# A four-layer network on one core: the wait of 52 slot writes, and the place of 14 small VectorE operations

## The chip, the cores and the metric

The kernel runs on one core of a Trainium2 chip. The metric is the device time of one execution in microseconds (us). TensorE (PE) multiplies matrices, VectorE (DVE), ScalarE (ACT) and GpSimd (POOL) do the elementwise work, and transfers are issued from SyncE (SP), ScalarE and GpSimd. Indirect transfers, whose target rows are taken from a table, are issued from GpSimd.

## The reference

There are 2048 tokens (4 sequences of 512) of width 512, and four blocks in a row, each added to its input: a selective scan over a context, a mixture of 32 experts with 4 per token, cross attention, and a second mixture of 32 experts with 8 per token. The change lies in the second mixture. Cut to what matters, it is:

```
x = layernorm(x)
scores = sigmoid(x @ router_w)                       # 2048 x 32
masked = the scores + bias of the 4 best of 8 groups of experts
top_k_index = top_k(masked, 8)
tkw = scores[top_k_index]; tkw = 2.5 * tkw / sum(tkw)
xs = repeat(x, 8)[argsort(experts)]                  # 16384 rows, expert by expert
down = (silu(xs @ w_gate) * (xs @ w_up)) @ w_down    # each row with its expert's weights
routed = sum over a token's 8 rows of down * tkw
shared = silu(x @ sw_gate) * (x @ sw_up) @ sw_down
out = residual + routed + shared
```

## The kernel before

The second mixture has two stages, one after the other with a barrier between: `route_stage` (with L = 1) and `expert_stage1`.

The routing stage computes the router's scores, picks the experts, and gives each of the 16384 pairs of token and expert a slot in a buffer in HBM, `xs1`. The slots of an expert are consecutive and padded to halves of 64 rows; two halves make a tile of 128 rows, and there are 144 tiles. `tcum` is the running count of halves up to each expert. TensorE meanwhile computes the shared expert: for each of four batches `b` of 512 tokens four chunks (`chunk(b, f)`, a gate and an up product), whose results VectorE multiplies (`product(b, f)`, line 1004), and then `down(b)` (line 1265), which needs all four products of its batch and whose four results VectorE adds to the residual (`add_shared(b)`, line 1066). VectorE does these between the steps of its own chain: the choice of experts, the slots of the first 512 tokens (`first_slots`), the table of experts per tile (`te`, `tei`), and the slots of the other three batches (`slots_of(b)`). Each engine executes its instructions in the order in which they are written.

The rows are written to their slots by 128 indirect transfers from GpSimd, each of 128 rows of 529 float32 (271 KB): 16 tiles of tokens times the 8 experts of a token. `SLOT_ORDER` puts the first batch of tokens first (32 writes), and then, for all other tokens, the 8 ranks one after another, starting with the lowest expert number, 12 writes a rank. The first 76 writes (`EARLY`) are issued in the routing stage, the last 52 at the start of the expert stage (line 1904). Write `n` raises the counter of lane `n % 4`. Before it issues write `n`, GpSimd waits until write `n - reach` has landed; `reach` is 2 in the routing stage and 3 in the expert stage.

The expert stage works through the 144 tiles. ScalarE issues the loads of rows, four tiles (a group) at a time, into two buffers; VectorE turns them (line 2058); TensorE multiplies with the gate and up weights (`up`, line 2141), turns the hidden rows (line 2150) and multiplies with the down weights (`down`, line 2163); ScalarE scales the result into one of 16 output tiles `e_yo` (line 1965); GpSimd adds its two halves to the output in HBM by two indirect transfers (line 1911). GpSimd does this only after all 128 slot writes have landed:

```
for n in range(EARLY, len(SLOT_ORDER)):
    write_slots(pool, D, route, n, 3)
for lane in range(LANES1):
    pool.wait_ge(written[lane], 16 * NT * K1 // LANES1)
```

Tile `t` takes the place of tile `t - 16`. VectorE (`addressed`, line 2087) therefore waits on the counter `added`, which GpSimd raises when it comes to the add of the tile two further on and finds the older adds landed. The adds of the first three tiles wait for one another; later ones wait only where halves of two experts meet.

The rows of the first six groups may not be loaded before enough slot writes have landed. How many is enough depends on how many experts lie in the group's rows: VectorE counts them from `tcum` into the table `rows_held` (14 operations on a single partition, lines 1190 to 1197), and ScalarE reads the table before each of these loads (`rows_written`). For the routing of these inputs the six groups need 56, 68, 80, 92, 104 and 116 writes.

SyncE loads the weights of the experts, one expert ahead of a ring of four, when the expert whose place they take is done.

Of the kernel before, what the change touches and what calls it, by code (L numbers as in the profile page):

```python
# [17 lines left out]
ALU = mybir.AluOpType  # L18
# [683 lines left out]
    step(dve.tensor_tensor(gt, gt, eq, ALU.add))  # L702


def write_slots(pool, D, route, n, reach):

    t, k = SLOT_ORDER[n]
    written = route["written"]
    if n >= reach:
        pool.wait_ge(written[(n - reach) % LANES1], 16 * ((n - reach) // LANES1 + 1))  # L710
    pool.indirect_dma_start(D["xs1"][:, :], bass.IndirectOffsetOnAxis(route["scat"][:, t, k:k + 1], 0),  # L711
                            route["xn"][:, t, 0:H + 2 * K1 + 1], None, bounds_check=NSLOT1 - 1, oob_is_err=False)\
        .then_inc(written[n % LANES1], 16)


def route_stage(nc, c, I, D, x, L, route, ahead=None, out=None):
# [10 lines left out]
    with ExitStack() as ctx:  # L727
# [79 lines left out]
        with nc.Block() as block:  # L807
# [65 lines left out]
            def _(pool):  # L873
# [14 lines left out]
                if L == 0:  # L888
                    for t in range(NT):
                        pool.wait_ge(sem["idx"], 1 + t // TB + 1)  # L890
                        for k in range(K):
                            n = t * K + k
                            if n >= 2:
                                pool.wait_ge(written[(n - 2) % LANES], 16 * ((n - 2) // LANES + 1))
                            pool.indirect_dma_start(slots[:, :], bass.IndirectOffsetOnAxis(scat[:, t, k:k + 1], 0),
                                                    xn[:, t, 0:XU], None, bounds_check=nslot - 1, oob_is_err=False)\
                                .then_inc(written[n % LANES], 16)
                    for lane in range(LANES):
                        pool.wait_ge(written[lane], 16 * NT * K // LANES)
                else:  # L900
                    for n in range(EARLY):
                        if n < TB * K and n % K == 0:
                            pool.wait_ge(sem["idx0"], 1 + n // K + 1)
                        if n == TB * K:
                            pool.wait_ge(sem["idx"], 1 + B - 1)
                        write_slots(pool, D, route, n, 2)

            @block.scalar
            def _(act):
# [49 lines left out]
            def _(dve):  # L959
# [188 lines left out]
                if L == 1:  # L1148
# [6 lines left out]
                    step(dve.tensor_scalar(route["ends"][0:1, 1:], ti[0:1, :], 1, None, ALU.arith_shift_right), wait=False)  # L1155
                    step(dve.tensor_scalar(te[:, :], te[:, :], float(E - 1), None, ALU.min))
                    dve.tensor_copy(tei[:, :], te[:, :]).then_inc(sem["eid"], 1)
                if L == 0:
                    slots_of(0, base1, lambda: product(0, FIRST + 2))
                    dve.wait_ge(sem["gate"], 1 + 1)  # L1160
# [18 lines left out]
                else:  # L1179
# [7 lines left out]
                    product(1, 3)  # L1187
                    slots_of(3, base1)
                    add_shared(1)
                    for g in range(GROUPS_HELD):  # L1190
                        step(dve.tensor_scalar(past[0:1, :], tcum[0:1, :], float(2 * RING1 * (g + 1) - 1), None, ALU.is_le))
                        step(dve.tensor_reduce(tf[0:1, g:g + 1], past[0:1, :], AX_X, ALU.add))
                    held = tf[0:1, 0:GROUPS_HELD]
                    per_rank = 16 * TB * (B - 1) // LANES1
                    step(dve.tensor_scalar(held, held, float(K1 - 1), None, ALU.min))
                    step(dve.tensor_scalar(route["rows_held"][:, :], held, float(per_rank), float(16 * TB * K1 // LANES1 + per_rank),
                                           ALU.mult, ALU.add), wait=False)
                    for b in range(2, B):
                        for f in range(FC):
                            product(b, f)  # L1200
# [606 lines left out]
def expert_stage1(nc, c, I, D, x, route, W, out):  # L1807
# [3 lines left out]
    with ExitStack() as ctx:  # L1811
# [59 lines left out]
        with nc.Block() as block:  # L1871
# [26 lines left out]
            def _(pool):  # L1898
# [2 lines left out]
                pool.iota(after_i[:, :], [[32, NTILE1 // 2], [32, 2], [0, 2]], base=-32, channel_multiplier=0).then_inc(sem["iota"], 1)  # L1901
                pool.iota(within_i[:, :], [[32, NTILE1 // 2], [0, 2]], base=0, channel_multiplier=0).then_inc(sem["iota"], 1)
                for n in range(EARLY, len(SLOT_ORDER)):
                    write_slots(pool, D, route, n, 3)
                for lane in range(LANES1):
                    pool.wait_ge(written[lane], 16 * NT * K1 // LANES1)
                pool.wait_ge(stored, 16 * (B + 2))
# [1361 lines left out]
```

## Time and profile before

| | us |
|---|---|
| three runs | 2952.52, 2956.33, 2965.47 |
| median | 2956.33 |
| the profiled execution | 2952.52 |
| its span | 2950.8 |

| engine | busy, us | share of the span |
|---|---|---|
| TensorE | 2628.0 | 89% |
| VectorE | 1542.0 | 52% |
| GpSimd | 1295.0 | 44% |
| ScalarE | 1032.9 | 35% |

The span is the time from the first to the last instruction in one profiled execution. The second mixture's routing stage begins near 1881 us, its expert stage near 2093 us. Of an issued transfer, an engine's row shows the issuing alone; how long it takes to land is seen only from who waits for it. "issue" as a releaser is time in which the engine waited for nothing that the profile shows.

### The profile page before, as it was taken

Reading aid. Unit: us, or ns where it says so; the run is one execution under the profiler, and the core shown is the slowest. Engines: PE = TensorE matmul, PEld = TensorE weight load, DVE = VectorE, ACT = ScalarE, POOL = GpSimd, SP = SyncE. Lnnn points to the kernel's source line nnn. Section 1 sums busy time; section 2 is a strip of 40 time slices with the busy share of each in tenths; the row PEclk is TensorE's granted clock in tenths of the full one; section 3 lists DMA queues with packets and bytes.
Section 4 is the critical chain, followed back from the end, with each engine's and each line's share of the span. In section 5 each row is a group of like instructions: output and inputs, shape, how many; then the busy total and the mean of one; then the engine's idle time right before and its main releaser. Section 6 shows DMA issues by size and latency. Waiting matters only on the chain. (4 is left out here: it accounts for less than half of the span.)

```text
span 2950.8 us, 40989 instructions
## 1 busy us (share of the span) xinstructions
PE 2628.0 (89%) x11315; PEld 1086.3 (37%) x11318; DVE 1542.0 (52%) x2668; ACT 1032.9 (35%) x1305; POOL 1295.0 (44%) x933
## 2 busy tenths in 40 slices
PE   5889876699999987768999999899798999999997
PEld 2333432244444433323343333334233333333332
DVE  7999999741100033126566665451344555555553
ACT  4647464120000001013443433200244555555553
POOL 2767656312400022114664643135445556545556
PEclk8999999999999999889999999899899999999999
DMA  3333222301210269975047300144786877787865
GB/s 127 116 98 109 83 62 74 130 36 37 88 33 14 73 218 343 340 205 141 1 121 200 96 1 1 51 175 169 214 233 131 166 157 128 160 199 162 171 115 79
DMA packets 361927, 373.15 MB, mean 126 GB/s; under 512 B 85810, under 2 KB 268403, under 8 KB 361778
## 3 DMA queue, kind: packets, MB, share of 16 engines
q1 hardware_dynamic: 202210, 239.03, 25.8%
q0 software_dynamic: 45520, 93.26, 14.9%
q10 hardware_dynamic: 114048, 39.16, 6.7%
q8 instruction: 58, 0.95, 0.1%
q14 instruction: 91, 0.75, 0.1%
HBM read 231.96 MB, written 152.14 MB: 130 GB/s over the span
## 5 line engine op out<-in xcount | busy, mean ns | idle before, releaser
L1911 POOL DMA_INDIRECT out_x<-e_yo,e_dest x288 | 418.9, 1455 | 327.7 <-DMA out_x<-e_yo,e_dest 249.7
L2141 PE MATMUL e_psg<-e_wgu,e_xsT 128*64 x1152 | 522.3, 596 | 17.0 <-DVE e_xsT L2058 17.0
L2141 PE MATMUL e_psg<-e_cgu,e_xsT 128*64 128x512 f32 x1152 | 522.3, 596 | 0.0
L295 POOL TENSOR_TENSOR hc<-hs,bcst 128x1024 f32<-128x1024 f32 x128 | 300.8, 2351 | 179.0 <-DVE ps_b L515 171.5
L640 PE MATMUL ps_y<-hc,ident 128*128 128x512 f32 x512 | 241.1, 609 | 88.1 <-POOL hc L295 87.8
L1984 ACT ACTIVATE e_cgu<-e_wgu 128x2048 f32 x144 | 275.2, 1912 | 66.2 <-issue 63.1
L521 DVE TENSOR_TENSOR_SCAN hs<-dA,ps_b 128x1024 f32<-128x1024 f32 x128 | 292.6, 2286 | 8.1 <-ACT dA L425 3.9
L2163 PE MATMUL e_pso<-e_wd,e_hT 128*64 x576 | 272.2, 595 | 14.8 <-DVE e_hT L2063 13.1
L2163 PE MATMUL e_pso<-e_cd,e_hT 128*64 128x512 f32 x576 | 272.2, 595 | 0.0
L2141 PEld LDWEIGHTS e_psg<-e_wgu,e_xsT 128*64 128x64 f32 x1152 | 154.7, 138 | 268.2 <-issue 268.1
L937 ACT ACTIVATE r_sg<-r_ps_g 128x512 f32<-128x512 f32 x60 | 35.8, 597 | 525.2 <-PE r_ps_g L1246 512.6
L1265 PE MATMUL r_ps_t<-r_wd,r_h 128*128 128x512 f32 x480 | 210.9, 600 | 9.4 <-DVE r_h L1004 5.1
L1004 DVE TENSOR_TENSOR r_h<-r_ps_u,r_sg 128x512 f32<-128x512 f32 x60 | 41.4, 691 | 316.7 <-PE r_ps_u L1246 299.6
L711 POOL DMA_INDIRECT slots_in<-r_xn,scat x128 | 126.9, 992 | 173.1 <-DMA slots_in<-r_xn,scat 101.2
L425 ACT ACTIVATE dA<-dt,a_neg 128x511 f32<-128x511 f32 x256 | 165.2, 713 | 102.9 <-DVE hs L521 97.8
L2751 DVE TENSOR_REDUCE a_nm<-a_ps 128x2 f32<-128x992 f32 x128 | 146.1, 1185 | 88.3 <-PE a_ps L2995 87.9
L2513 ACT ACTIVATE a_pt<-a_ps 128x1024 f32<-128x1024 f32 (+1 forms) x128 | 126.2, 1022 | 181.3 <-PE a_ps L3012 120.5
L2068 DVE TENSOR_TENSOR e_h<-e_psg,e_sg 128x256 f32<-128x256 f32 x144 | 61.1, 424 | 244.0 <-ACT e_sg L1958 212.8
L640 PEld LDWEIGHTS ps_y<-hc,ident 128*128 128x128 f32 x512 | 92.8, 191 | 231.1 <-POOL hc L295 137.4
L1965 ACT ACTIVATE e_yo<-e_pso,e_wrow 128x512 f32<-128x512 f32 x144 | 99.0, 688 | 223.9 <-PE e_pso L2163 176.0
L2058 DVE STREAM_TRANSPOSE e_xsT<-e_xs 128x512 f32<-128x512 f32 x144 | 173.0, 1201 | 5.8 <-DMA e_xs<-slots_in 5.8
L2076 DVE COPY e_cd<-e_wd 128x1024 f32 x144 | 102.0, 708 | 133.7 <-PE e_pso L2163 107.7
(430 smaller groups left out, 4207.0 us busy)
## 6 DMA issues: line engine op xcount, KB each, us to landing
slots_in<-zeros SPq DMA_DIRECT2D x144, 256.0 KB, 2.3
e_xs<-slots_in ACTq DMA_DIRECT2D x144, 256.0 KB
bcst<-bc_rows SPq DMA_DIRECT2D x128, 256.0 KB, 4.2
e_wgu<-in_wg SPq DMA_DIRECT2D x32, 512.0 KB
e_wgu<-in_wu SPq DMA_DIRECT2D x32, 512.0 KB
e_wd<-in_wd SPq DMA_DIRECT2D x32, 512.0 KB
e_w<-in_wg SPq DMA_DIRECT2D x11, 1408.0 KB
e_w<-in_wu SPq DMA_DIRECT2D x11, 1408.0 KB
```

The lines of the kernel that those rows point to most:

```text
L295: pool.tensor_tensor(hc[:, it % 2, half(h), :], hs[:, it % 2, half(h), :], bc(bcst[:, q, 1, :], 1, HB), ALU.mult).then_inc(sem["hc"], 1)
L425: i = act.activation(dA[:, it % 2, t, 1:], dt[:, b % 2, t, 1:], ACT.Exp, scale=a_neg[:, n, t:t + 1])
L521: dve.tensor_tensor_scan(hs[:, it % 2, half(h), :].rearrange(flat), dA[:, it % 2, half(h), :].rearrange(flat), ps_b[:, :, :].rearrange(fla ...
L640: i = pe.matmul(ps_y[:, t, :], c["ident"][:, :], hc[:, it % 2, t, :], start=False, stop=False, skip_group_check=True)
L711: pool.indirect_dma_start(D["xs1"][:, :], bass.IndirectOffsetOnAxis(route["scat"][:, t, k:k + 1], 0), route["xn"][:, t, 0:H + 2 * K1 + 1], ...
L1265: i = pe.matmul(ps_t[:, j % 2, :], h[:, f, j * P:(j + 1) * P], wd[:, f, :], start=f == 0, stop=f == FC - 1)
L1911: pool.indirect_dma_start(out[:, :], bass.IndirectOffsetOnAxis(dest[:, q, s:s + 1], 0), yo[half(s), q, :], None, bounds_check=T + 2 * P - ...
L1984: act.activation(cgu[:, q % 2, :, :], wgu[:, bass.ds(e % RING, 1), :, :].rearrange("p o k n -> p (o k) n"), ACT.Copy).then_inc(sem["cgu"], 1)
L2058: dve.transpose(xsT[:, q % 2, :, :].rearrange("p k (s j) -> p k s j", j=DQ), xs[:, q // RING % 2, part, :].rearrange("p s (i k) -> p k s i ...
L2141: j = pe.matmul(ps_g[half(s), q % 2, :], xsT[:, q % 2, k, half(s)], w, start=k == 0, stop=k == KH - 1, tile_position=(0, s * HALF), skip_g ...
L2163: j = pe.matmul(ps_o[half(s), q % 2, :], hT[:, q % 2, a, half(s)], w, start=a == 0, stop=a == NW - 1, tile_position=(0, s * HALF), skip_gr ...
L2751: dve.tensor_reduce(nm[:, i % 8, 2 * z:2 * z + 2], ps[:, at:at + 2, 0:S2], AX_X, ALU.max, negate=True)\
```

## The change

Two things are edited. `write_slots` loses its parameter `reach`: all 128 writes now wait for the second write before. And the 14 operations that fill `rows_held` are written directly behind the one that hands over the table `tei`, in place of behind `add_shared(1)`.

```
-def write_slots(pool, D, route, n, reach):
+def write_slots(pool, D, route, n):
...
-    if n >= reach:
-        pool.wait_ge(written[(n - reach) % LANES1], 16 * ((n - reach) // LANES1 + 1))
+    if n >= 2:
+        pool.wait_ge(written[(n - 2) % LANES1], 16 * ((n - 2) // LANES1 + 1))
...
-                        write_slots(pool, D, route, n, 2)
+                        write_slots(pool, D, route, n)
...
                     dve.tensor_copy(tei[:, :], te[:, :]).then_inc(sem["eid"], 1)
+                    for g in range(GROUPS_HELD):
+                        step(dve.tensor_scalar(past[0:1, :], tcum[0:1, :], float(2 * RING1 * (g + 1) - 1), None, ALU.is_le))
...
                 if L == 0:
...
                     add_shared(1)
-                    for g in range(GROUPS_HELD):
-                        step(dve.tensor_scalar(past[0:1, :], tcum[0:1, :], float(2 * RING1 * (g + 1) - 1), None, ALU.is_le))
...
                     for b in range(2, B):
...
-                    write_slots(pool, D, route, n, 3)
+                    write_slots(pool, D, route, n)
```

On GpSimd, at the start of the expert stage, before the change (`e_sloti` to `e_withini` are number tables; the counters of the four lanes stand under the names `m_win`, `m_weights`, `m_xin` and `m_ctxin`, in the order of lanes 0 to 3):

```order
L1901 IOTA e_afteri 1x288
L1902 IOTA e_withini 1x144
L711 DMA slots_in<-r_xn,scat 18432x544 [waits m_weights]
L711 DMA slots_in<-r_xn,scat 18432x544 [waits m_xin]
L711 DMA slots_in<-r_xn,scat 18432x544 [waits m_ctxin]
L711 DMA slots_in<-r_xn,scat 18432x544 [waits m_win]
```

On GpSimd, at the same place, in the changed kernel:

```order
L1901 IOTA e_afteri 1x288
L1902 IOTA e_withini 1x144
L711 DMA slots_in<-r_xn,scat 18432x544 [waits m_xin]
L711 DMA slots_in<-r_xn,scat 18432x544 [waits m_ctxin]
L711 DMA slots_in<-r_xn,scat 18432x544 [waits m_win]
L711 DMA slots_in<-r_xn,scat 18432x544 [waits m_weights]
```

The writes are the same and stand in the same order; each, from number 76 on (lane 0), waits for the lane two behind its own in place of three.

On VectorE, in the routing stage behind the table `tei`, before the change (`r_te` and `r_tei` are that table, `r_h` the products of the shared expert, `r_seg`, `r_k` and `r_hit` the slots of batch 1):

```order
L1156 TENSOR_SCALAR r_te<-r_te 128x3
L1157 CAST r_tei<-r_te 128x3
L1004 TENSOR_TENSOR r_h<-r_ps_u,r_sg 128x512 x2
L1011 TENSOR_TENSOR r_seg<-r_pos,r_base 128x128
L1018 COPY r_seg<-r_sc 128x128
```

On VectorE, at the same place, in the changed kernel (the last of the six pairs of lines 1159 and 1160, and what follows):

```order
L1159 TENSOR_SCALAR r_past<-r_tcum 1x32
L1160 TENSOR_REDUCE r_tf<-r_past 1x1
L1163 TENSOR_SCALAR r_tf<-r_tf 1x6
L1164 TENSOR_SCALAR rows_held<-r_tf 1x6
L1004 TENSOR_TENSOR r_h<-r_ps_u,r_sg 128x512 x2
L1011 TENSOR_TENSOR r_seg<-r_pos,r_base 128x128
L1018 COPY r_seg<-r_sc 128x128
```

The two products of batch 0, `product(0, 2)` and `product(0, 3)`, now stand behind 14 more operations.

## Rows read from the trace of the kernel before

**Rows 1.** The page's chain that ended last, by line, shares of the span.
```profile
PE e_psg L2141 12%; PE e_pso L2163 6%; DMA out_x<-e_yo,e_dest 2%; PE e_psh L2150 1%; POOL out_x L1911 0%; POOLq L1939 0%; POOLq L1937 0%; POOLq L1928 0%; POOLq L80 0%; POOLq L1911 0%; DVE e_xsT L2058 0%; DMA slots_in<-r_xn,scat 0%; ACT e_yo L1965 0%; POOLq L79 0%; DVEq L2072 0%
```

**Rows 2.** Stretches: us, busy us by engine, granted PE clock, DMA share, GB/s.
```profile
core 0: us, PE busy (x) PEld busy (x) DVE busy (x) ACT busy (x) POOL busy (x), PEclk, DMA share, GB/s
2214.00:2226.00 12.00, 0.42 (x4) 0.30 (x4) 2.83 (x8) 0.38 (x1) 3.90 (x3) 0.67 0.31 36
2300.00:2900.00 600.00, 600.00 (x3442) 231.24 (x3440) 321.23 (x862) 320.36 (x323) 331.17 (x228) 1.00 0.77 155
```

**Rows 3.** VectorE in order of time: start us, us, what, [idle before <-releaser].
```profile
2222.03 0.23 DVE L2087 SCALAR_TENSOR_TENSOR e_mine<-e_rec,e_slot 128x8 f32<-128x8 f32 x1 [12.65 <-POOLq L1932]
```

**Rows 4.** TensorE in order of time, at the same place.
```profile
2225.66 1.11 PE L2163 MATMUL e_pso<-e_wd,e_hT 128*64 x1 [11.58 <-DVE e_hT L2063]
```

**Rows 5.** The chain of waits, 2190 to 2225 us: start us, us, what.
```profile
2196.76 6.38 issue
...
2217.94 3.74 DMA out_x<-e_yo,e_dest
```

**Rows 6.** GpSimd in order of time: slot writes of the expert stage.
```profile
2095.22 1.01 POOL L711 DMA_INDIRECT slots_in<-r_xn,scat  x1 [0.18 <-issue]
...
2102.62 0.98 POOL L711 DMA_INDIRECT slots_in<-r_xn,scat  x1 [3.81 <-DMA slots_in<-r_xn,scat]
...
2172.13 0.98 POOL L711 DMA_INDIRECT slots_in<-r_xn,scat  x1 [0.30 <-issue]
2173.42 0.98 POOL L711 DMA_INDIRECT slots_in<-r_xn,scat  x1 [0.30 <-issue]
...
2195.78 0.98 POOL L711 DMA_INDIRECT slots_in<-r_xn,scat  x1 [0.31 <-issue]
```

**Rows 7.** GpSimd in order of time: slot writes of the routing stage.
```profile
1947.36 0.98 POOL L711 DMA_INDIRECT slots_in<-r_xn,scat  x1 [3.54 <-DMA slots_in<-r_xn,scat]
1952.09 0.98 POOL L711 DMA_INDIRECT slots_in<-r_xn,scat  x1 [3.75 <-DMA slots_in<-r_xn,scat]
1954.31 0.98 POOL L711 DMA_INDIRECT slots_in<-r_xn,scat  x1 [1.24 <-issue]
...
2003.01 0.98 POOL L711 DMA_INDIRECT slots_in<-r_xn,scat  x1 [2.56 <-DMA slots_in<-r_xn,scat]
...
2082.00 0.98 POOL L711 DMA_INDIRECT slots_in<-r_xn,scat  x1 [0.76 <-DMA slots_in<-r_xn,scat]
2083.82 0.98 POOL L711 DMA_INDIRECT slots_in<-r_xn,scat  x1 [0.84 <-DMA slots_in<-r_xn,scat]
```

**Rows 8.** Stretches with slot writes, columns as in rows 2.
```profile
1942.00:1968.00 26.00, 25.21 (x52) 11.07 (x53) 10.60 (x30) 0.60 (x1) 7.98 (x9) 0.88 0.88 306
2073.00:2084.00 11.00, 11.00 (x27) 4.93 (x26) 2.07 (x3) 0.00 (x0) 6.07 (x7) 1.00 0.38 145
2095.00:2120.00 25.00, 15.51 (x72) 5.47 (x74) 9.92 (x24) 8.99 (x7) 10.08 (x11) 0.72 1.01 258
```

**Rows 9.** VectorE in order of time, in the routing stage.
```profile
1941.40 1.29 DVE L1004 TENSOR_TENSOR r_h<-r_ps_u,r_sg 128x512 f32<-128x512 f32 x2
...
1993.79 0.20 DVE L1038 COPY r_xn<-r_k 128x32 f32<-128x32 f32 x1
...
2002.56 0.16 DVE L1191 TENSOR_SCALAR r_past<-r_tcum 1x32 f32<-1x32 f32 x1
...
2005.30 0.16 DVE L1196 TENSOR_SCALAR rows_held<-r_tf 1x6 int32<-1x6 f32 x1
2008.87 0.69 DVE L1004 TENSOR_TENSOR r_h<-r_ps_u,r_sg 128x512 f32<-128x512 f32 x1 [3.41 <-PE r_ps_u L1246]
```

**Rows 10.** TensorE in order of time, `down(0)` and `down(1)`.
```profile
1942.79 16.80 PE L1265 MATMUL r_ps_t<-r_wd,r_h 128*128 128x512 f32 x32 [3.37 <-issue]
...
1987.91 14.00 PE L1265 MATMUL r_ps_t<-r_wd,r_h 128*128 128x512 f32 x32 [0.85 <-DVE r_h L1004]
```

**Rows 11.** GpSimd's first operation in the expert stage.
```profile
2092.83 0.24 POOL L1899 IOTA e_sloti<- 128x144 int32 x1 [8.03 <-POOLq L112]
```

**Rows 12.** ScalarE's queue: the loads of rows that it issues in tile 10.
```profile
2172.50 0.99 ACTq L1970 DMA_DIRECT2D e_xs<-slots_in  x2
```

More of the change, by code:

```diff
@@ L1157, in _ @@
                     dve.tensor_copy(tei[:, :], te[:, :]).then_inc(sem["eid"], 1)
+                    for g in range(GROUPS_HELD):
+                        step(dve.tensor_scalar(past[0:1, :], tcum[0:1, :], float(2 * RING1 * (g + 1) - 1), None, ALU.is_le))
+                        step(dve.tensor_reduce(tf[0:1, g:g + 1], past[0:1, :], AX_X, ALU.add))
+                    held = tf[0:1, 0:GROUPS_HELD]
+                    per_rank = 16 * TB * (B - 1) // LANES1
+                    step(dve.tensor_scalar(held, held, float(K1 - 1), None, ALU.min))
+                    step(dve.tensor_scalar(route["rows_held"][:, :], held, float(per_rank), float(16 * TB * K1 // LANES1 + per_rank),
+                                           ALU.mult, ALU.add), wait=False)
                 if L == 0:
@@ L1189, in _ @@
                     add_shared(1)
-                    for g in range(GROUPS_HELD):
-                        step(dve.tensor_scalar(past[0:1, :], tcum[0:1, :], float(2 * RING1 * (g + 1) - 1), None, ALU.is_le))
[L1192 to L1197, printed above, removed]
                     for b in range(2, B):
```

## The prediction

> **What bounds the kernel now.** I read four views in this order: the chain of waits, the stretches of the last stage, the order of time around its one long stall, and the order of time of the slot writes that stand behind that stall.
>
> The chain that ended last runs through TensorE in the routed experts of layer 1 [rows 1]. From 2300 to 2900 us TensorE is busy all of the time, 600.00 of 600.00 us, at a granted clock of 1.00 [rows 2]; a tile has 32 of its instructions, so the 3442 are 107.6 tiles of 5.58 us. Nothing there can be gained or lost except at the end. So what happens ahead of 2300 us is passed on to the end one for one, if it delays TensorE. In the stretch from 2214 to 2226 TensorE works 0.42 of 12 us [rows 2]. VectorE is idle for 12.65 us before `e_mine` of tile 16, released by GpSimd's line 1932 [rows 3], and TensorE's next `e_pso` then starts after 11.58 us idle, released by VectorE's `e_hT` [rows 4]. Line 1932 is the count `added`: tile 16 takes the place of tile 0 in the ring of 16 output tiles and needs tile 0's two adds, and GpSimd raises the count only when it comes to tile 2. GpSimd comes to its first add so late because it must first issue all 128 slot writes and see them land. The chain says so: 6.38 us from the last write to GpSimd's next step, then adds, one after another, the fourth at 2217.94 [rows 5]. Thus the end of the slot writes is on the path, with no slack: whatever is added to it, up to tens of us, TensorE waits for at tile 16, and whatever is taken away comes back only up to the 11.58 us stall.
>
> **Edit 1, the wait of the last 52 slot writes on the second write before, in place of the third.** The 52 writes of the last stage start at 2095.22 and the last at 2195.78: 51 steps in 100.56 us, 1.97 us each [rows 6]. Undisturbed, a step lasts 1.29 us there (2172.13 to 2173.42), the price of issuing alone, so three writes in flight cover the whole way to landing. Of the 51 steps 27 are of this kind (under 1.36 us); the other 24 wait for a landing, and all steps together lie 34.8 us above 51 x 1.29. The first 76 writes, in the routing stage, already wait for the second before: there the undisturbed step is 1.78 to 1.82 us, as from 2082.00 to 2083.82 [rows 7]. Two such steps, 3.56 us, are the time from a write's start to the start of the write that waits for it. So the floor of the new order is 51 x 1.78 = 90.8 us.
>
> On that floor come the disturbances. They are latencies, seen under loads of rows and weights: DMA share 1.01 at 2095 to 2120 us, against 0.38 at the clean writes [rows 8]. With three in flight 2095.22 to 2102.62 took 7.40 us from a write to the one that waits for it [rows 6]. With two in flight and a DMA share of 0.88 [rows 8], two steps are nearly as long: from 1947.36 over 1952.09 to 1954.31 they make 6.95 us [rows 7]. The latency in traffic thus hardly shrinks with one write less in flight, and two in flight share it by 2 and not by 3. I replayed the 52 starts: where a write's step was over 1.36 us, the latency of the third before it is the difference of their starts; elsewhere it is 3.56 us, or less where the next starts force it. Under a wait on the second before, latencies kept whole make 136.8 us (+36.2); the part over 3.56 us scaled by 0.8, 127.1 us (+26.5); by two thirds, 120.7 us (+20.2); by a half, 112.9 us (+12.3); no excess at all, 90.3 us (-10). Adding only the part of each old step that is over 1.78 us to the floor gives 115 us (+14.5). The latest consistent latencies everywhere give 153 us (+52.5). The value that I take is 122 us, +21.5: latencies in traffic almost whole, less what the last ten or so writes gain, which now start when TensorE has stopped and its rows and weights are no longer loaded.
>
> From the Trainium skill, DMA: Bandwidth & Descriptors, section "Queues, rings and completion order": a DMA engine serves its queue rows in turn, a packet at a time. By that rule the latency of a write in traffic is made by the other queues and stays when fewer writes are in flight, and the sum would take the +36.2 us of the replay; the 6.95 us with two in flight [rows 7] agrees.
>
> Behind the last write, the 6.38 us to GpSimd's next step [rows 5] were in full traffic. A clean landing is 3.56 us from the start of the write, 2.58 us from the end of its 0.98 us of issuing, so up to 3.8 us come back; I take -2. The four adds behind stand as they are: 4.5 us apart, waiting for each other's landing, not for traffic. TensorE's stall grows from 11.6 to over 30 us. The clock after such a stall is read from rows: after 11.58 us idle the first product pairs go at half clock, mean granted 0.67 over 2214 to 2226 [rows 2], and after the pause ahead of this stage TensorE also starts at half clock. I take +1 for a longer slow start, bounds 0 and +2.6.
>
> Other waiters of the same counts: ScalarE asks for a part of the writes before it loads rows of groups 2 to 5 (80, 92, 104 and 116 writes for these inputs' routing), in tiles 2, 6, 10 and 14. Tile 10's loads are issued at 2172.50 [rows 12], tile 14's four tiles of 5.6 us later or more. In my replay the 104th write starts near 2167 us and the 116th near 2196 us, each a little before it is asked for; a wait of some us there would stop TensorE only in time that it otherwise spends waiting at tile 16. I count nothing; with latencies kept whole it would be up to 10 us, still hidden.
>
> **Edit 2, 14 small VectorE operations moved forward.** They count the experts of each group of rows. Before, they run from 2002.56 to 2005.46, 2.90 us, and VectorE then is idle 3.41 us until TensorE has a product: there they cost nothing, so taking them away gives nothing [rows 9]. Now they stand ahead of `product(0, 2)`, which starts at 1941.40 straight behind the operation before it [rows 9]. VectorE is late there: TensorE's `down(0)` starts at 1942.79 after 3.37 us idle [rows 10], because it needs the products of all four chunks. So 2.90 us go fully onto TensorE, whose work from there to the end of the stage has only gaps under 1 us. The end of the stage shifts with it: GpSimd's own writes of the first part are issued by 2084.80 [rows 7], yet its part of the last stage begins at 2092.83, after 8.03 us idle [rows 11]; GpSimd doesn't hold the change of stage, and starts 2.9 us later. The first expert weights are issued behind the id table, which isn't moved. Write 33, which waits for `slots_of(3)`, starts at 2003.01 [rows 7]; its table is done at 1993.99 [rows 9] and would be at 1996.9: 6 us of cover. TensorE's `down(0)` took 16.80 us at half clock for a part against 14.00 us for the next one [rows 10]; a longer gap may move that by 2 us either way, taken as 0. Edit 2: +2.9, bounds 0.9 and 4.9.
>
> **Sum.** +21.5 - 2 + 1 + 2.9 = +23.4 us. The profiled execution took 2952.52 us (span 2950.8), so 2976; the median of the three runs shown is 3.8 us above that one, and half of this makes the predicted 2978. A measurement of this kernel tells about 0.5%, 14.8 us, from no change.
>
> **The rivals.**
>
> *The writes were held by their own number.* If the latency in traffic is the queueing of a write behind its own two predecessors, one fewer in flight shortens it in proportion. The place is the stretch of 52 writes; the price is the floor, 90.3 us, 10 us less than now, and with edit 2 and the slow start the end comes at 2952.5 - 10 + 3.9 = 2946. It decides when the excess of latency falls below about a quarter of what it was, where the replay crosses 100.6 us. At the mean pace of the first 76 writes, 2.02 us a step, it would be 103 us and 2959. For it: a DMA share of 1.01 says throughput and not latency. Against it: 6.95 us with two in flight.
>
> *Latencies kept whole.* 136.8 us, perhaps 153: +36 to +52, with edit 2 and the clock 2992 to 3008. For it: the pairs in traffic of the first block. Against it: the last writes now run in quiet time.
>
> *A write lands in less than two issues.* Then the second before has landed whenever the next can be issued, edit 1 costs nothing, and only edit 2 is left: 2952.5 + 2.9 = 2955. Against it: the clean steps of 1.78 us in place of 1.29 [rows 6, 7], seen at a DMA share of 0.38. The Trainium skill, DMA: Bandwidth & Descriptors, section "Anatomy of one DMA", fits a GpSimd DMA as 2.0 us plus its bytes by 436 GB/s; for 271 KB an estimate of 2.6 us, which is this rival. The trace disagrees, with 3.56 us.
>
> *The path isn't as read.* If tile 16 is held by something other than the end of the writes, both edits hide: no change, 2953 to 2958. The chain of waits speaks against it.
>
> **Chances.** Forecast, +15 to +31 us (2967 to 2984): 0.57. Latencies whole or more: 0.21. Own number, at the floor or the first block's pace: 0.15. Landing in two issues: 0.02. Path misread: 0.05. The forecast's own low edge is just at the 0.5% bound, and some of its weight (0.04) falls inside. So slower 0.76, the same 0.22, faster 0.02. The range that leaves out about a tenth on each side is 2957 to 3002.
>
> **What the changed profile would show.** The 14 operations in one row near 1941 us and `down(0)` near 1945.7; GpSimd's last stage starting near 2095.7; undisturbed steps of 1.78 us between the 52 writes and a last start near 2220, not 2196; TensorE idle over 30 us in tile 16, and from there the same 5.58 us a tile to the end. A last write before 2200 would show the own-number rival; a stall at tile 16 as short as before, with late writes, would show that the path was misread; `down(0)` unmoved would refute edit 2's price.

## The result, and the profile after

| | before | after |
|---|---|---|
| median, us | 2957.26 (2952.52 to 2965.47) | 2981.47 (2976.76 to 2982.8) |
| the profiled execution, us | 2952.52 | 2986.22 |
| its span, us | 2950.8 | 2984.5 |

The change makes the kernel slower: ratio 1.0083, 95% interval 1.0067 to 1.0099, or 20 to 29 us. Forecast were 2978 us, 2957 to 3002, and 0.76 for slower. The profiled execution after is not one of the four behind the median. It is one of fifteen executions of the changed kernel on record, 2976.76 to 2988.6 us with a median of 2982.8, and lies 4.8 us above the median in the table.

GpSimd's slot writes of the expert stage after the change, in order of time (start us, us, what, [idle before <-releaser]), answer to [rows 5, 6, 11]:

```profile
2099.12 0.24 POOL L1899 IOTA e_sloti<- 128x144 int32 x1 [8.03 <-POOLq L112]
...
2101.50 1.01 POOL L711 DMA_INDIRECT slots_in<-r_xn,scat  x1 [0.18 <-issue]
2102.82 0.98 POOL L711 DMA_INDIRECT slots_in<-r_xn,scat  x1 [0.30 <-issue]
2109.15 0.98 POOL L711 DMA_INDIRECT slots_in<-r_xn,scat  x1 [5.35 <-DMA slots_in<-r_xn,scat]
...
2233.17 0.98 POOL L711 DMA_INDIRECT slots_in<-r_xn,scat  x1 [1.60 <-DMA slots_in<-r_xn,scat]
2234.79 0.98 POOL L711 DMA_INDIRECT slots_in<-r_xn,scat  x1 [0.64 <-issue]
2238.58 1.50 POOL L1911 DMA_INDIRECT out_x<-e_yo,e_dest  x1 [2.81 <-issue]
```

The 52 writes start from 2101.50 to 2234.79, 133.3 us in place of 100.6. The third write of the row starts 7.65 us after the first, on which it waits. With three in flight the fourth started 7.40 us after the first [rows 6]: the latency is the same, and now two writes share it. Behind the issuing of the last write GpSimd's first add starts after 2.81 us; before it was 7.34 us (2196.76 to 2204.10).

VectorE's row and TensorE's in tile 16 answer to [rows 3] and [rows 4]:

```profile
2256.44 0.23 DVE L2087 SCALAR_TENSOR_TENSOR e_mine<-e_rec,e_slot 128x8 f32<-128x8 f32 x1 [31.26 <-POOLq L1932]
```

```profile
2260.07 1.11 PE L2163 MATMUL e_pso<-e_wd,e_hT 128*64 x1 [30.20 <-DVE e_hT L2063]
```

The same line 1932 releases it, after 31.26 us in place of 12.65, and TensorE stands for 30.20 us in place of 11.58. The chain of waits has the adds as before, one behind the other's landing, up to that line:

```profile
2234.79 0.98 DMA slots_in<-r_xn,scat
2235.77 1.85 issue
...
2252.43 3.65 DMA out_x<-e_yo,e_dest
...
2256.19 0.03 POOLq L1932
```

The stretches (us, busy us by engine, PE clock, DMA share, GB/s) answer to [rows 2]:

```profile
2226.00:2260.00 34.00, 3.88 (x26) 1.25 (x20) 2.62 (x8) 2.98 (x3) 12.29 (x10) 0.61 0.33 73
2300.00:2900.00 600.00, 600.00 (x3438) 232.21 (x3436) 322.30 (x858) 319.93 (x323) 339.19 (x231) 1.00 0.79 159
```

TensorE works 3.88 of 34 us around the stall, and stops at 2229.87 us (its row starts at 2260.07 after 30.20 us idle). Only the last three writes (2230.59, 2233.17 and 2234.79) start behind that. From 2226 to 2236 us the DMA share is still 0.52, and from 2236 to 2256 it is 0.26. From 2300 to 2900 us TensorE is busy all of the time as before, 3438 instructions against 3442. Nothing is given back there.

Edit 2 is seen where it was expected. VectorE and TensorE in the routing stage, against [rows 9] and [rows 10]:

```profile
1946.66 0.16 DVE L1159 TENSOR_SCALAR r_past<-r_tcum 1x32 f32<-1x32 f32 x1
...
1949.43 0.16 DVE L1164 TENSOR_SCALAR rows_held<-r_tf 1x6 int32<-1x6 f32 x1
1949.51 1.29 DVE L1004 TENSOR_TENSOR r_h<-r_ps_u,r_sg 128x512 f32<-128x512 f32 x2
```

```profile
1950.90 2.04 PE L1265 MATMUL r_ps_t<-r_wd,r_h 128*128 128x512 f32 x2 [6.22 <-issue]
```

The 14 operations take 2.85 us from the first start to the product's, and the idle time ahead of `down(0)` grows from 3.37 to 6.22 us, by 2.85. Yet of this hardly anything reaches the start of the expert stage: its first write stands 164.16 us from the first slot write, against 163.15. Over five kernels whose routing stage is that of the kernel before, this distance scatters from 160.75 to 164.65 us, so 1.0 us is no more than scatter.

The two profiled executions differ by 33.7 us, and the difference can be added up from the starts. Ahead of the first slot write (1932.07 and 1937.34) lie 5.3 us, which is no part of the change: over the runs that point scatters from 1927.7 to 1940.1, and the medians differ by 24.2 us only. From there to the first write of the expert stage 1.0 (163.15 and 164.16); the 52 writes 32.7; from the last write's issue to the first add -4.5; from that add to `e_mine` of tile 16 nothing (17.93 and 17.86); from there to the end -0.7.

### The profile page after: what moved, and what is told of

Read it like the earlier page. It is cut to its first block and busy times, and to the rows that moved or that the text cites. A ratio compares the mean times of both kernels' runs of the same rounds, so it can differ in the third digit from the quotient of the medians.

```text
span 2984.5 us, 40991 instructions
## 1 busy us (share of the span) xinstructions
PE 2638.7 (88%) x11317; PEld 1091.7 (37%) x11318; DVE 1544.1 (52%) x2668; ACT 1032.0 (35%) x1305; POOL 1297.2 (43%) x933
## 6 DMA issues: line engine op xcount, KB each, us to landing
e_w<-in_wg SPq DMA_DIRECT2D x11, 1408.0 KB, 17.2
e_w<-in_wu SPq DMA_DIRECT2D x11, 1408.0 KB, 18.1
```

## The experiments

All distances called "from the first write" are from the start of the first of the 128 slot writes in the same execution, since that start itself scatters. Times are medians. Ratios are to the kernel before, as recorded with their 95% interval; they are not the quotient of the two medians. The kernel before had a median of 2957.44 us beside the first four experiments, 2955.62 beside the next four and 2958.11 beside the last three. Readings of a trace are of one execution.

### Each edit alone

Edit 1 alone:

```
-                    write_slots(pool, D, route, n, 3)
+                    write_slots(pool, D, route, n, 2)
```

> Edit 1 alone: the last 52 slot writes wait for the second write before, the 14 small VectorE operations stay where they were. My theory (latency in traffic is made by other transfers, and the end of the writes holds tile 16): about 21 us slower than before, 2978, that is all of the measured 24 but the 1 to 3 us of edit 2; steps of the writes sum to about 133 us against 100.6; TensorE's stall at tile 16 near 31 us. Rival (edit 2 or an interplay of the two made the difference): under 12 us slower.

Measured 2981.83 us, 1.0073 (1.005 to 1.0096). The 52 writes take 132.6 us, and TensorE's stall at tile 16 is 31.64 us. The time lies 24.4 us above that of the kernel before, and the whole change had 24.2. That is the whole change.

Edit 2 alone: the 14 operations behind the `tei` copy, the 52 writes waiting for the third before.

> Edit 2 alone: the 14 operations stand ahead of product(0, 2), the last 52 writes wait for the third before. My theory: down(0) starts 2.9 us later and the start of the expert stage with it, so +1 to +3 us, 2958 to 2960, within what the measurement tells from no change. Rival (the moved operations cost as much as the writes): +10 us or more. Second rival (they are hidden): the expert stage starts at the same distance from the first slot write as before, 160.8 us.

Measured 2954.99 us, 0.9987 (0.9972 to 1.0001): no cost. `down(0)` starts after 6.74 us idle, so the delay is there, but the first write of the expert stage stands 163.25 us from the first write, against 163.15. The 2.9 us of the sum are lost on the way. GpSimd's first row of the stage, and VectorE's last row of the routing stage, say where:

```profile
2096.22 0.24 POOL L1899 IOTA e_sloti<- 128x144 int32 x1 [8.51 <-POOLq L112]
```

```profile
2093.11 0.69 DVE L1066 TENSOR_TENSOR x_resid<-r_ps_t,x_resid 128x512 f32<-128x512 f32 x1 [2.74 <-PE r_ps_t L1265]
```

GpSimd's idle time ahead of the stage is 8.03 us before, after, and in three more kernels, and 8.51 in edit 1's and edit 2's: it is counted from GpSimd's own last write of the routing stage. That speaks for GpSimd as the one that holds the change of stage. With edit 2 alone, however, the stage also starts 3.11 us behind the start of VectorE's last add, and further down this is the mark of a stage that VectorE holds. The two marks fall together here: the move has used up all of the cover, but the stage doesn't start later.

The 52 writes took 94.4 us in this kernel, with the order of the kernel before, which took 100.6. In the three other kernels with 52 writes on the third before, the lengths are 99.5, 100.6 and 101.3 us. So a row of one execution is known to some 6 us. The earlier end brought nothing here either: ScalarE stood 10.64 us ahead of 2179.49, and the time is that of the kernel before.

### More and fewer writes in flight

```
-                    write_slots(pool, D, route, n, 3)
+                    write_slots(pool, D, route, n, 4)
```

> The kernel before with the last 52 writes waiting for the fourth write before, in place of the third. If latency in traffic is made by the other transfers and does not grow with the number in flight, the stretch of 52 writes shrinks from 100 us towards 51 x 1.29 = 66 plus stalls, near 85 us; the stall at tile 16 (11.6 us) vanishes and the time is 8 to 13 us under the kernel before, 2945. Rival, own number: the latency grows by a third with the fourth in flight, the stretch stays at 100 us and the time the same, 2957.

```
-                    write_slots(pool, D, route, n, 3)
+                    write_slots(pool, D, route, n, 1)
```

> The kernel before with each of the last 52 writes waiting for the one just before it: one in flight. If latency does not depend on the number in flight, the stretch is the sum of the latencies: a clean write 3.56 us, in traffic 5 to 7, so about 52 x 4.3 = 225 us (the later ones run clean, since TensorE stands still), and the time is about 120 us over before, 3075. Rival, own number: a lone write in traffic takes no more than a clean one, 51 x 3.6 = 184 us, +80, 3037.

With one in flight: 3068.47 us, 1.0362 (1.0326 to 1.0399). The 52 writes take 218.6 us and TensorE stands 51.93 us in tile 16. Its GpSimd in order of time, first in traffic (DMA share 0.46 at 2130 to 2150 us), then undisturbed:

```profile
2135.52 0.99 POOL L711 DMA_INDIRECT slots_in<-r_xn,scat  x1 [2.75 <-DMA slots_in<-r_xn,scat]
2143.53 0.98 POOL L711 DMA_INDIRECT slots_in<-r_xn,scat  x1 [7.02 <-DMA slots_in<-r_xn,scat]
...
2305.47 0.98 POOL L711 DMA_INDIRECT slots_in<-r_xn,scat  x1 [2.60 <-DMA slots_in<-r_xn,scat]
2309.07 0.98 POOL L711 DMA_INDIRECT slots_in<-r_xn,scat  x1 [2.62 <-DMA slots_in<-r_xn,scat]
```

Undisturbed, a write needs 3.60 us from its start to the start of the one that waits for it, as two steps of 1.78 us did with two in flight [rows 7]. In traffic one took 8.01 us with no other slot write in flight, and the first write of the row 7.60 us, against 7.65 with one more behind it, 7.40 with two (6.90 in edit 2 alone) and 7.68 with three. The row of 218.6 us is also far above the 184 us that the rival gave it. So the latency is not mainly the queueing of a write behind its own predecessors, and the rival "held by their own number" is out as an account of the change.

That latency is wholly the same at any number in flight is not shown. The prediction's replay, fed with the latencies of the kernel before, gives 136.8 us for two in flight (measured 133.3 and 132.6), 82.8 for four (86.4), but 253.7 for one (218.6); these are estimates from the starts. Only 11 of the 51 lone writes took over 5 us. Much of their row stands in quiet time, while TensorE waits for rows, and how much of the 35 us comes from that stays open. From the Trainium skill, DMA: Bandwidth & Descriptors, "Queues, rings and completion order": a DMA engine serves its queue rows in turn. These 8.01 us, with no other slot write in flight, agree with it; whose packets they waited for is in no row.

With four in flight the 52 writes take 86.4 us, but the time is 2959.18 us, 1.0006 (0.9985 to 1.0027). The row is as short as the theory had it, near 85 us, but the time isn't its 2945. The 14 us are lost before they reach tile 16. ScalarE and TensorE of that kernel in order of time, with the writes beside them:

```profile
2165.38 1.91 ACT L1984 ACTIVATE e_cgu<-e_wgu 128x2048 f32 x1
2190.11 0.38 ACT L1958 ACTIVATE e_sg<-e_psg 128x256 f32<-128x256 f32 x1 [22.81 <-remote]
```

```profile
2170.97 1.11 PE L2163 MATMUL e_pso<-e_wd,e_hT 128*64 x1 [6.55 <-issue]
2191.00 1.12 PE L2150 MATMUL e_psh<-ident,e_h 128*64 128x128 f32 x8 [16.35 <-DVE e_h L2068]
```

```profile
2164.86 1.43 POOL L711 DMA_INDIRECT slots_in<-r_xn,scat  x1 [0.30 <-issue]
2166.59 0.98 POOL L711 DMA_INDIRECT slots_in<-r_xn,scat  x1 [0.30 <-issue]
...
2185.86 0.98 POOL L711 DMA_INDIRECT slots_in<-r_xn,scat  x1 [0.31 <-issue]
2189.66 1.50 POOL L1911 DMA_INDIRECT out_x<-e_yo,e_dest  x1 [2.81 <-issue]
```

While GpSimd issues one write after another with 0.30 us between them, ScalarE stands 22.81 us in a wait that ends on no counter of the kernel, and goes on 3.3 us after the issuing of the last write (2186.84). TensorE's two stalls there, 6.55 and 16.35 us, are more than the 11.58 us of tile 16, which are gone; its idle time from the first product of the stage on is 24.2 us against 19.1 before. And the chain of waits has 24.66 us in that place:

```profile
2165.43 24.66 another core or an unknown queue
```

The DMA share is 0.54 from 2165 to 2187 us, so the DMA engines weren't full. Such waits of ScalarE (with the releaser `remote`) between the start of the stage and tile 16 sum to 7.6 us before (2.83 and 4.75), and there are none in the three runs with two or one in flight.

### The same order in the routing stage

These two, one with the 14 operations moved, were to bring GpSimd's 76 writes to an earlier end and so to uncover edit 2:

```
-                        write_slots(pool, D, route, n, 2)
+                        write_slots(pool, D, route, n, 3)
```

> The kernel before with all 128 slot writes waiting for the third before, in the routing stage too. Theory A (found in the traces: the expert stage starts 8.0 to 8.5 us after GpSimd's 76th write is issued, whatever VectorE does): the 76 writes hold the change of stage, so the expert stage starts earlier, until VectorE holds it; from the first slot write to the first of the expert stage 160 to 162 us in place of 163.2, GpSimd's 76th write 10 us or more earlier. Time 1 to 3 us less, 2955. Theory B (the prediction's): GpSimd doesn't hold it, and the distance stays 163.2.

> As the kernel with all 128 writes on the third before, and the 14 VectorE operations moved ahead of product(0, 2) too. Theory A (GpSimd's 76 writes covered edit 2): without that cover the move costs its 2.9 us: the expert stage starts 2.5 to 3.5 us later after the first slot write than in the twin without the move. Theory B (the move is free by itself): the two start at the same distance, within 0.5 us.

Measured 2968.75 us, 1.0051 (1.003 to 1.0073), and with the move 2979.4 us, 1.0087 (1.0066 to 1.0108). GpSimd does end early: its 76 writes take 120.7 and 124.0 us in place of 151.8. But the expert stage starts 18 us later, 180.91 and 181.29 us from the first write, so both theories of the first run missed. VectorE of the first of the two shows why:

```profile
2050.89 0.69 DVE L1066 TENSOR_TENSOR x_resid<-r_ps_t,x_resid 128x512 f32<-128x512 f32 x1 [15.34 <-remote]
2062.10 1.29 DVE L1066 TENSOR_TENSOR x_resid<-r_ps_t,x_resid 128x512 f32<-128x512 f32 x2 [10.53 <-remote]
```

These are waits with the same releaser on another engine, 26 us in all, and the last write starts at 2057.02. Of edit 2 the pair tells nothing: the two distances agree within 0.4 us, as the second theory of the second run has it, but VectorE's stalls are not the same in both (16.73 and 7.04 us with the move) and hold the stage in either. Why the median with the move is 10.7 us higher isn't shown.

### More writes early, and writes in rows with pauses

```
-EARLY = 76
+EARLY = 92
...
-                        write_slots(pool, D, route, n, 2)
+                        write_slots(pool, D, route, n, 3)
```

> As the kernel with all writes on the third before, with 92 in place of 76 of them issued in the routing stage, 36 in the expert stage. If the end of the writes holds tile 16, it comes near 2172 and not 2204, the stall at tile 16 (11.6 us) is gone and no other replaces it but short waits of ScalarE for instructions: 2943, 0.5% under before. Rival (while writes are issued back to back ScalarE and VectorE stand still in waits that no semaphore of the kernel ends, 22.8 us with four in flight): that takes the place of the stall, 2955 or more.

Measured 2967.41 us, 1.0059 (1.0039 to 1.0079). With 36 writes left for the expert stage there is no stall at tile 16, and TensorE's idle time from the first product of that stage on falls from 19.1 to 4.2 us; from its first write to the end it takes 20 us less. The routing stage takes 32 us more (195.12 us from the first write), again by VectorE:

```profile
2050.04 0.69 DVE L1066 TENSOR_TENSOR x_resid<-r_ps_t,x_resid 128x512 f32<-128x512 f32 x1 [18.14 <-issue]
2072.45 0.69 DVE L1066 TENSOR_TENSOR x_resid<-r_ps_t,x_resid 128x512 f32<-128x512 f32 x1 [21.72 <-remote]
```

and GpSimd beside it:

```profile
2048.41 0.98 POOL L711 DMA_INDIRECT slots_in<-r_xn,scat  x1 [0.30 <-issue]
2050.03 0.98 POOL L711 DMA_INDIRECT slots_in<-r_xn,scat  x1 [0.65 <-DMA slots_in<-r_xn,scat]
...
2073.18 0.98 POOL L711 DMA_INDIRECT slots_in<-r_xn,scat  x1 [0.30 <-issue]
```

The first of the waits (its releaser isn't named) ends together with the only pause in a row of writes that lasts from before 2032 to 2074 us (0.65 us in place of 0.30), the second between the starts of the last two. The theory missed the time, as it counted nothing for the routing stage; the rival had the time right, but with the waits on VectorE there, and none on ScalarE in the expert stage.

```
-                    write_slots(pool, D, route, n, 3)
+                    write_slots(pool, D, route, n, 1 if n % 8 == 4 else 4)
```

> The kernel before, its last 52 writes waiting for the fourth before, but every eighth for the one just before it, so that the issuing pauses 6 times. If an unbroken row of writes starves what ScalarE and VectorE wait for in the waits that end on nothing of the kernel's (7.6 us with three in flight, 22.8 with four, none with two), they vanish or stay under 5 us here, and the writes take about 100 us as before: 2950 to 2957. If those waits come from the number in flight and not from the missing pauses, they stay near 20 us.

Measured 2957.97 us, 1.0013 (1.0002 to 1.0023). The writes take 102.3 us, so the pauses give back what four in flight had won. ScalarE's waits of the kind fall from 22.8 to 11.7 us, which lies between the two theories. They are three waits of 4.08, 3.98 and 3.62 us in place of one, and each ends in a pause, 1.1 to 1.5 us after the issuing of the last write ahead of it. The profiled execution is the slowest of the ten, 8.5 us above the median.

### GpSimd out of the way of edit 2

```
-EARLY = 76
+EARLY = 60
```

with the two orders of waiting as before, and the same with the 14 operations moved:

> The kernel before with EARLY = 60 in place of 76: 60 slot writes (second before) in the routing stage, 68 (third before) in the expert stage. It takes away GpSimd's part in holding the change of stage. Theory (GpSimd's 76 writes hold the change of stage, VectorE and TensorE are done some 3 us sooner): GpSimd's 60th write starts some 32 us sooner, about 120 us after the first one, and its idle time ahead of the expert stage grows to some 37 us; but the stage starts only about 3 us sooner, so that its first write stands 158 to 161 us after the first write of all (163.15 in the kernel before). Rival (something else holds the change of stage, GpSimd only happens to end near it): 163 us as before. The last write comes some 27 us after the 2195.78 of before (68 writes of 1.97 us, 134 us), and with it TensorE's stall at tile 16: 2952.5 + 27 to 29 = about 2980 us.

> The same with EARLY = 60 and the 14 operations moved as in the change. Read against the run with EARLY = 60 alone, by the distance from the first slot write to the first one of the expert stage, with GpSimd out of the way. Theory (edit 2 costs 2.9 us of VectorE's time, which only GpSimd's 76 writes hid): the distance is 2.9 us longer (bounds 2 to 4), and so is the whole time. Rival (TensorE and VectorE make up for the 2.9 us by themselves, in the gaps between their own steps, until the stage ends): the same distance within 1 us.

Measured 2980.94 us, 1.0077 (1.0055 to 1.01), and with the move 2978.23 us, 1.0073 (1.0048 to 1.0099). GpSimd's start of the expert stage, without and with the move:

```profile
2094.80 0.24 POOL L1899 IOTA e_sloti<- 128x144 int32 x1 [29.89 <-POOLq L112]
```

```profile
2094.34 0.24 POOL L1899 IOTA e_sloti<- 128x144 int32 x1 [37.41 <-POOLq L112]
```

The first write of the stage stands 157.18 us from the first write (1940.01 to 2097.19) and with the move 163.11 us (1933.61 to 2096.72). So with GpSimd gone the stage starts 6.0 us sooner than before (158 to 161 us were forecast), and the move costs 5.9 us there (2 to 4 were forecast). Of these, `down(0)` explains all: without the move it took 13.97 us after 3.37 us idle, with it 16.92 us after 6.36 us. Thus 3.0 us are the later start and 2.95 us a half clock for a part of it. The latter is no clear cost of the move: `down(0)` took 16.1 to 17.0 us in all five kernels with the move, but without it also 16.4 to 16.8 us in six of eight, the kernel before among them [rows 10], and 14.0 us in two. The start of VectorE's last add, counted from the first write, sorts the kernels with two in flight in the routing stage the same way: 154.4 to 154.5 us in four without the move, 151.7 in the two whose `down(0)` took 14.0 us, 157.6 to 157.8 in three with the move. So at equal clock the move costs VectorE's end 3.2 us.

In the whole time the 5.9 us aren't seen, as with 68 writes left the expert stage has other stalls, 40.5 us of TensorE's idle time without the move and 33.7 with it. The last write is there 7 us sooner than expected without the move (the 68 take 119.0 us, with it 123.4); the time came out as forecast only because ScalarE stood elsewhere: 13.09 us ahead of 2117.73 and 12.19 us ahead of 2143.29, both released by a slot write, and 17.20 us ahead of 2208.20 in a wait of the kind found with four in flight.

```
+                    for copy in range(4):
                         (the 14 operations, ahead of product(0, 2))
```

> The kernel with the move alone (third before in the expert stage, 14 operations ahead of product(0, 2)), and the row of 14 written four times there: 11.6 us in place of 2.9. Theory (GpSimd hides about 3 us and no more): down(0) begins 8.7 us later after its release than with one row (idle some 15 us, against 6.74), and the first write of the expert stage stands 5.6 to 8.7 us further from the first write of all than the 163.25 us of the move alone, 169 to 172 us; the whole time is 2955 + 6 to 9 = 2961 to 2964. Rival (the stages' own gaps take it in): at most 3 us, 163 to 166 us, and 2955 to 2958.

Measured 2962.74 us, 1.0014 (0.9996 to 1.0031). `down(0)` begins after 15.01 us idle, 8.3 us more than with one row. GpSimd, then VectorE's last `add_shared`:

```profile
2084.88 0.98 POOL L711 DMA_INDIRECT slots_in<-r_xn,scat  x1 [1.29 <-DMA slots_in<-r_xn,scat]
2097.81 0.24 POOL L1900 IOTA e_sloti<- 128x144 int32 x1 [11.95 <-POOLq L112]
```

```profile
2094.71 0.69 DVE L1066 TENSOR_TENSOR x_resid<-r_ps_t,x_resid 128x512 f32<-128x512 f32 x1 [2.74 <-PE r_ps_t L1266]
```

(A line was added, so line 1900 is 1899 of the others; the last row is of the engine's last add.) GpSimd's idle time is now 11.95 us and no longer 8.03 or 8.51: it waits for VectorE, and the first write of the stage stands 171.05 us from the first write (1929.15 to 2100.20), 7.8 us further than in the move alone; the median is 7.75 us above the move's. The start of `e_sloti` is 3.10 us behind the start of VectorE's last add here, and 3.10 and 3.11 in the two kernels with 60 early writes. In the kernel before it is 6.24, in the changed one 4.19:

```profile
2086.59 0.69 DVE L1066 TENSOR_TENSOR x_resid<-r_ps_t,x_resid 128x512 f32<-128x512 f32 x1 [2.74 <-PE r_ps_t L1265]
```

```profile
2094.93 0.69 DVE L1066 TENSOR_TENSOR x_resid<-r_ps_t,x_resid 128x512 f32<-128x512 f32 x1 [2.74 <-PE r_ps_t L1265]
```

So VectorE had 3.1 us of slack before, 1.1 after and none with edit 2 alone: GpSimd held the change of stage before, and its cover was about as long as the 3.2 us of the move. The cover scatters from one execution to the next. GpSimd's 76th write starts 149.4 to 152.8 us from the first in the kernels that wait for the second before, apart from this last one, and with the routing stage of the kernel before the slack was 2.8 to 3.1 us in three traces, 0.8 in one, and 7.4 in the one with the short `down(0)`. That 1.1 us were left in the changed kernel is due to a 76th write that starts 1.0 us later there.

## Why the prediction was right, and which of its steps failed

*What bounds the kernel: right.* The end of the slot writes holds tile 16 through `added`, with no slack. In the change and in edit 1 alone the stall there grows by 18.6 and 20.1 us, and the time by what the end of the writes slips; the rest of the slip is taken by TensorE's waits ahead of tile 16, below.

*Edit 1: right in kind, too small.* The term was +21.5 us and measured +32.7 (+32.0 in edit 1 alone). From three in flight to two the latencies in traffic stay whole to within 4 us of the row, 7.65 us against 7.40 at its start. The 14.7 us that were cut from the replay's +36.2 were worth 3.5 to 4.2. They were cut for "what the last ten or so writes gain, which now start when TensorE has stopped". But TensorE stopped at 2229.87 us, and only three writes started behind that (four in edit 1 alone, where it stopped at 2223.04). The rows of single executions scatter by some 6 us, so the size of the miss, 11 us, is known to no more than that. One reading was loose: the 6.95 us in [rows 7] end on "issue", so they only bound that latency from above. The step from 1942.84 to 1952.09, 9.25 us, did end on a landing. The rival "latencies kept whole" had the term right to 3.5 us, and its time of 2992 to 3008 wrong by the other terms.

*The landing behind the last write:* -2 taken, -4.5 measured. The bound of -3.8 was counted from a clean landing of 3.56 us against 6.38 us of one row of the chain, and the whole way to the first add was 7.34 us before and 2.81 after.

*The slower start of the clock:* +1 taken, none found; from `e_mine` of tile 16 to the end it is 728.8 us before and 728.1 after.

*ScalarE's waits for the 92nd, 104th and 116th write:* right. Behind its loads of rows ScalarE comes to `e_yo` after 6.46, 5.06 and 10.59 us idle, at 2155.37, 2181.07 and 2213.01. I read these as the waits, since the slot writes that wait for the 92nd, 104th and 116th start at 2155.08, 2180.51 and 2212.77, 0.2 to 0.6 us ahead; the profile names a slot write as the releaser of the first only. TensorE's 3.1, 2.1 and 7.9 us of idle time near them are inside what tile 16 would have waited anyway, since the sum closes without them.

*Edit 2: the term failed.* The step of it that failed is "GpSimd doesn't hold the change of stage, and starts 2.9 us later". The first half of the step was right: the move delays `down(0)` by 2.85 us and VectorE's last add by 3.1 to 3.2. But the 8.03 us of idle time in [rows 11] were read as slack of GpSimd; they are the way from its last write to the next stage, and 3.1 us of slack were VectorE's. Of the sum, the writes were 11.2 us too low, and edit 2 (measured at +1.0 at most), the clock and the landing together 6.1 us too high: +23.4 against +28.4 in the two traces behind the first slot write, and +24.2 in the medians. The forecast of 2978 us lies 3.5 us under the measured 2981.5. The direction and the main cause were foreseen; that the number came so near is luck in part, as a term that was 11 us too low met three that were 6 us too high, and behind the first slot write the two traces differ by 4 us more than the medians.

*Own number:* refuted by the run with one in flight (218.6 us against its 184). *A landing in two issues:* refuted by 3.60 us, undisturbed, with one in flight. The prediction set the estimate of 2.6 us against these whole 3.56 us and said that the trace disagrees. Counted from the end of the issuing the landing took 2.58 us, which agrees; the estimate just leaves out the 0.98 us of issuing. *Path misread:* refuted by the stall at tile 16, which grew with the end of the writes.

## What to carry to other kernels

A wait for "the n-th before" costs latency divided by n, and most where the latency is longest. Here the latency under load hardly changed from three in flight to two, so it had to be replayed whole. An engine that starts a stage after a constant idle time, counted from its own last instruction, may be the one that holds it: compare that time over two kernels before calling it slack, and compare the same distance for the other engines. And a delay put on one engine costs nothing up to the slack of that engine and nearly everything beyond. Here the slack was 3 us, and writing the row four times moved the stage by 7.8 of the 8.3 us of added delay.

## What the runs showed of the chip that was not expected

Rows of indirect transfers that GpSimd issues with 0.30 us between them go together with waits of ScalarE and VectorE that end on no counter of the kernel (releaser `remote`). Up to tile 16 such waits of ScalarE sum to 0 us in the three kernels with one or two in flight in the expert stage, 3.1 to 17.2 in the seven with three and the 76 or 60 early writes, 22.8 with four and 11.7 with four and pauses. With three in flight and 92 early writes there are none. In the routing stage, where three were allowed, VectorE's long waits were 15.3 and 10.5 us, 16.7 and 7.0 with the move, and 18.1 and 21.7 with 92 early writes. The sums count by that label; a few of these waits, such as the 16.7 and the 18.1 us, have "issue" as their releaser.

What ends them is not shown. Some end in a pause or after the row, as with four in flight. Others end within an unbroken row, such as VectorE's 15.34 us at 2050.89 in the kernel with all writes on the third before:

```profile
2049.00 0.98 POOL L711 DMA_INDIRECT slots_in<-r_xn,scat  x1 [0.30 <-issue]
2050.28 0.98 POOL L711 DMA_INDIRECT slots_in<-r_xn,scat  x1 [0.30 <-issue]
2051.57 0.98 POOL L711 DMA_INDIRECT slots_in<-r_xn,scat  x1 [0.30 <-issue]
```

ScalarE's 17.20 us at 2208.20 (60 early writes) and 10.74 us at 2182.01 (the row of 14 four times) end so too.

A late load of the program comes to mind, and the profile doesn't bear it out. One transfer of the instruction queue lies in the 22.81 us with four in flight, and one in each of VectorE's 10.53, 16.73 and 18.14 us. None lies in VectorE's 15.34 and 21.72 us, nor in ScalarE's 17.20 and 10.74 us, nor in the 2.83 and 4.75 us of the kernel before. So the cause stays open. What is shown is the effect: more writes in flight end the writes sooner and gain nothing, and no version tried here is faster than the kernel before by more than its measurement can tell.
